# Products of zeros behind the first projection and the second conditioning are left out

## The reference

```python
# layer 0
h = x * rsqrt(mean(x**2)) * (ln1_w * (1 + cond @ ln1_tw.T))
q, k, v = h @ Wq.T, h @ Wk.T, h @ Wv.T      # 8 query heads, 1 key/value head of 64
q, k = rope(q), rope(k)
x = x + softmax(q @ k.T / 8) @ v @ Wo.T
h = x * rsqrt(mean(x**2)) * (ln2_w * (1 + cond @ ln2_tw.T))
x = x + (silu(h @ Wg.T) * (h @ Wu.T)) @ Wd.T # inner width 2048
# layer 1
scale, shift = split(cond @ W_ada.T + b_ada)
h = layernorm(x) * (1 + scale) + shift
q, c = h @ Wq1.T, h @ Wkd.T                  # 16 query heads of 32, latent 128
k, v = c @ Wku.T, c @ Wvu.T                  # 4 key/value heads
x = x + softmax(mask(rope(q) @ rope(k).T / sqrt(32))) @ v @ Wo1.T
```

## Time and profile before

| | |
|---|---|
| time, median of 3 runs | 905.38 us (902.44 to 907.66) |
| the profiled execution's own time | 901.88 us |
| its span, first to last instruction | 900.1 us |
| TensorE busy | 878.1 us (98%) |
| VectorE, ScalarE, GpSimd busy | 63%, 52%, 46% |
| mean granted TensorE clock | 0.998 of 2.4 GHz |
| HBM read, written | 67.96 MB, 4.19 MB |

### The profile page before, as it was taken

How to read it: one execution, slowest core, us unless ns; L and a number is a source line. 1 busy time by engine, 2 the same in 40 slices (tenths; PEclk the granted TensorE clock), 3 DMA queues, 4 the chain that set the end, 5 groups by cost and what they waited for, 6 DMA issues and landing times.

```text
span 900.1 us, 16086 instructions
## 1 busy us (share of the span) xinstructions
PE 878.1 (98%) x6190; PEld 736.7 (82%) x6190; DVE 569.8 (63%) x943; ACT 470.2 (52%) x862; POOL 414.8 (46%) x315
## 2 busy tenths in 40 slices
PE   8898999999999999999999999999999999998997
PEld 5787888888888888887887888888888888888885
DVE  5775556556556556567456676585774765757886
ACT  5666446455445445445537556455464464444662
POOL 3566545445435445446447545453444344431331
PEclk9999999999999999999999999999999999999999
DMA  9901222122222221122132222221222222100001
GB/s 343 333 24 40 103 81 82 71 82 83 71 83 83 71 82 72 71 71 88 71 117 71 71 71 83 71 83 52 68 83 71 83 83 71 69 3 13 25 25 36
DMA packets 31003, 73.19 MB, mean 81 GB/s; under 512 B 4304, under 2 KB 4816, under 8 KB 30928
## 3 DMA queue, kind: packets, MB, share of 16 engines
q1 hardware_dynamic: 30208, 72.07, 23.0%
q10 hardware_dynamic: 720, 0.09, 0.1%
HBM read 67.96 MB, written 4.19 MB: 80 GB/s over the span
## 4 chain that ended last, share of the span: by engine, by line
PE 83%; issue 6%; DVE 5%; POOL 4%; ACT 2%; DMA 0%; POOLq 0%; ACTq 0%; DVEq 0%
PE ps L484 25%; PE ps L486 24%; PE ps L485 24%; PE ps L763 2%; PE ps L590 1%; PE ps L572 1%; PE ps L741 1%; PE ps L751 1%; PE ps L557 1%; POOL qr L343 1%; PE ps L717 1%; POOL qr L395 1%; PE ps L690 1%; POOL stat L317 1%; POOL kr L394 1%
## 5 line engine op out<-in xcount | busy, mean ns | idle before, releaser
L360 POOL TENSOR_TENSOR gul<-rgu,guh 128x1024 fp32r<-128x1024 f32 x64 | 156.4, 2444 | 187.8 <-ACT guh L1453 187.8
L1067 DVE TENSOR_TENSOR xres<-ps,xres 128x512 f32<-128x512 f32 x256 | 174.6, 687 | 88.2 <-PE ps L486 88.2
L484 PE MATMUL ps<-h2h,guh 128*128 128x512 f32 x512 | 205.8, 402 | 0.7 <-issue 0.7
L486 PE MATMUL ps<-h2l,guh 128*128 128x512 f32 x512 | 199.7, 390 | 0.0
L485 PE MATMUL ps<-h2h,gul 128*128 128x512 f32 x512 | 199.5, 390 | 0.0
L486 PEld LDWEIGHTS ps<-h2l,guh 128*128 128x128 f32 x512 | 96.1, 188 | 20.8
L484 PEld LDWEIGHTS ps<-h2h,guh 128*128 128x128 f32 x512 | 96.2, 188 | 20.3 <-issue 1.1
L485 PEld LDWEIGHTS ps<-h2h,gul 128*128 128x128 f32 x512 | 96.3, 188 | 18.7
L484 PE MATMUL ps<-wdh,ah 128*128 128x512 f32 x256 | 101.0, 394 | 1.2 <-DVE al L1062 1.2
L1475 ACT CAST ah<-af 128x512 fp32r<-128x512 f32 x64 | 39.7, 621 | 119.2 <-DVE af L1080 119.2
L486 PE MATMUL ps<-wdl,ah 128*128 128x512 f32 x256 | 99.8, 390 | 0.0
(11 more groups left out here) (172 smaller groups left out, 1688.7 us busy)
## 6 DMA issues: line engine op xcount, KB each, us to landing
rgu<-gu SPq DMA_DIRECT2D x64, 512.0 KB, 3.6
rwd<-WdT SPq DMA_DIRECT2D x64, 256.0 KB, 2.7
xt<-xT SPq DMA_DIRECT2D x16, 256.0 KB, 3.1
out<-xres SPq DMA_DIRECT2D x15, 256.0 KB, 2.3
xres<-x SPq DMA_DIRECT2D x1, 2560.0 KB, 16.2
adaw<-adaT SPq DMA_DIRECT2D x1, 2048.0 KB, 10.3
wst<-WqkvT SPq DMA_DIRECT2D x4, 320.0 KB, 6.0
adaw<-ln_twT SPq DMA_DIRECT2D x4, 256.0 KB, 4.2
```

Of the source, the lines that this page charges most:

```text
L360: pool.tensor_tensor(gul[i][:, :], rgu[i][:, :], guh[i][:, :], ALU.subtract).then_inc(m_gul, 1)
L484: pe.matmul(dst, lh, rh, start=start, stop=False)
L486: return pe.matmul(dst, lh, rl, start=False, stop=stop)
L1067: dve.tensor_tensor(at, bank(BD[i % 2]), at, ALU.add).then_inc(m_x, 1)
```

## The change

Five products of zeros of the beginning are left out: the three behind the first projection and the two behind the second conditioning. Those in front of these places (the four at the start, one between the parts of the first conditioning, three behind its transpose) stay.

```diff
@@ -841,7 +841,6 @@
                     scores(s)
                 if s == -1:
                     first_qkv()
-                    keep_warm(3)
                 elif in_layer(s + 1):
                     qkv(s + 1)
                 if s <= HEAD and in_layer(s - 1):
@@ -853,8 +852,6 @@
                 if s == HEAD + 1:
                     project(s - 1)
                 condition_later(s)
-                if s == -1:
-                    keep_warm(2)
                 fill(pieces, f1)
                 if in_layer(s):
                     p_T(s)
```

## The result

| | before | after |
|---|---|---|
| median | 904.54 us (20 runs, 902.32 to 907.66) | 906.42 us (20 runs, 905.43 to 909.10) |
| ratio | | 1.0025 (95% interval 1.0017 to 1.0033) |
| profiled execution, own time | 901.88 us | 905.94 us |
| its span | 900.1 us | 904.1 us |
| its mean granted TensorE clock | 0.998 | 0.992 |

The change costs 0.25%: about 2.3 us by the ratio, 1.9 us by the medians.

What follows compares the result with a forecast made beforehand. TensorE, busy 98% of the span, was taken as the bound, though off the path where the products stood. Direct effect 0 plus 1.0 us of low clock on the 905.4 us median gave 906.4 us; range 902.5 to 910.

Steps and rivals of the forecast that it cites:

- No direct effect: Program start: the conditioning comes forward 0.0 to 0.5 us, the transposes still wait for GpSimd; gain on the chain 0.
- The clock falls after the longer idle piece: After 2.5 to 2.9 us idle before the first transposes, TensorE drops to 1.2 GHz, beginning between 18.5 and 22.3.
- The price of the low stretch, +1.0 us: First tile's chain: one 3.42 us low-clock stretch costs 0 to +1.3 us, taken as +1.0; two in a row +2.5.
- The first 0.2 us are free.: Second tile's projection: a delay of it alone hides 0.2 us behind VectorE's softmax product, which ends at 26.20.
- The transposes' share, between x1 and x1.8: First tile's transposes, 0.76 us at full clock, slow by x1 to x1.8 at low clock: 0 to +0.6 us.
- The delay passes on: Beyond 25.93 the second tile's rotation, GpSimd's sums and transposes at 30.56 inherit the delay; TensorE then ends late.
- Rival A: Program start: the clock never falls, so cost 0 and time 905.4 us; chance 0.20.
- The forecast: Whole kernel: one or two low-clock stretches, 0 to +2.5 us, expected +1.0, median 906.4 us; chance 0.65.
- Rival B: First tiles: low clock lasts from 20.24 beyond 27 without a break, +5 us, time 910.4; chance 0.10.
- my sign for B: Profile after: the low clock level being there beyond 27 us would show it staying low for several tiles.
- Rival C: First tile: GpSimd's sum L343 speeds up without the products beside it, 0.56 us back, time 904.8; chance 0.05.

Runs made afterwards that it cites:

- the second layer's place out of play: Seven identity products fill TensorE's 2.03 us idle piece at 822 us: kernel before with it 0.9984, changed kernel with it 1.0013, both against the kernel before.
- without the last two: Kernel before with only the two products of zeros behind the second conditioning left out: 1.0021, median 905.85 us.
- more products: Kernel before with five instead of two products of zeros behind the second conditioning: 0.9999, median 904.27 us.
- the changed kernel with the second place filled: Changed kernel with six identity products behind the third conditioning, ahead of the second tile's transposes, against the kernel before: 1.0009, median 906.13 us.

## Why the prediction was right, and where it was off

By the steps of the prediction:

- **No direct effect.** Right. The transposes started at 20.22 for 20.24, ScalarE's copy at 19.17 for 19.19, and the conditioning came forward to 16.22 and was released by its load, at the early one of the two ends that I gave.
- **The clock falls after the longer idle piece.** Right, and the experiments bear it out. In the five profiles with 2.7 us or more of idling ahead of the first transposes (2.71, 2.92, 2.95, 3.09, 4.01) the clock falls there; in the seven with 1.7 us or less it doesn't. Longer pieces mostly go with fewer products; what tells the two apart is that two products or none, with the same 2.9 us of idling, lose the same.
- **The price of the low stretch, +1.0 us.** Right in kind, too small in size. I took one stretch; the profile has two in a row, which I had priced at 2.5 us and which cost 2.69: transposes +0.43 (the copy of the queries starts at 21.47 for 21.04), scores +0.44 (22.11 to 23.17, for 21.68 to 22.30), projection +1.82 (23.17 to 28.62, for 22.30 to 25.93). In it the products stand 0.27 us apart (24.40 to 24.67, for 0.15).
- **"The first 0.2 us are free."** Wrong. Before, the rotation began 0.20 us after the projection's end, and after the change it began 0.20 us after its end too (28.82 - 28.62). What I read as the softmax's cover is the time from TensorE's last product to VectorE's start; both ends fell together by chance. In the sum this is 0.2 us at most.
- **The transposes' share, between x1 and x1.8.** L558 took 0.42 us for 0.27. The Trainium skill's rule ("TensorE: Matmul & The Clock Gate", Part 4), by which they would not change with the clock, does not hold here; by it 0.43 us of the 2.69 would be missing.
- **The delay passes on.** Right, and it grew, which I had not foreseen: 2.69 to 3.68 us at the third tile, by the low stretch at 33.9. Rival A's argument, that 1.78 us of idling behind dense work keep the clock, held for the kernel before and for the four others with that length; the four profiles with 2.05 us or more there all lose it. In the changed kernel that idle piece is 2.06 us, because the work in front of it is done sooner after the projection (the third conditioning starts 0.64 us behind the start of L503, for 0.91 before, when the transposes between them still had to wait for the softmax), while the chain through VectorE and GpSimd is as long as ever (28.82 to 33.25, for 26.13 to 30.56: 4.43 us in both).
- **The forecast.** 906.4 us against a measured 906.42. This agreement owes something to luck: I put +1.0 us on the median of three runs, 905.38, and the median of 20 is 904.54. Measured against that, the price was 1.9 us, 2.3 by the ratio, 2.6 with the second layer's place out of play. The step that failed is the number of low stretches: the term was one. The two profiles differ by three. Over all executions the mean clock is 0.9952 before and 0.9913 after, a difference of two stretches, and with the second layer's place filled it is 0.9970 and 0.9925, a difference of 2.4.
- **Rival B** (several tiles at the low level) did not happen, though not by much: the first low piece ended at 27.05, just where I had put the point from which it would decide, and read to the letter my sign for B, a low level beyond 27, was met by 0.05 us and by the stretch at 33.9. The clock did come back between the two. Only with the later stretch did the profile's loss come near the 4.5 us.
- **Rival C** (GpSimd's sum gets faster) did not happen: L343 takes 1.97 us with the products beside it and without them.

The Trainium skill ("TensorE: Matmul & The Clock Gate", "Terms") prices a low clock roughly as its time by the missing share. By that, as an estimate, the two stretches would cost 6.83 x 0.5 = 3.4 us. The trace shows 2.69: 0.68 us of the time is a wait, and the products slow down by less than a factor of two (the scores from 0.62 to 1.06 us, the projection's products from 0.15 to 0.27 us apart). What is not settled: how often the second tile's idle piece loses the clock in the mean of executions, why the same 2.03 us of idling in the second layer lose it in five profiles and keep it in four, and what decides over the low stretch at the program's end.

## What to carry to other kernels

That TensorE idles behind a product of zeros does not make the product free to take away: look at the granted clock behind the nearest idle piece of that length in the same trace, and price what hangs on the chain in the first microseconds after it. When such products stand behind one another with a load's wait between them, those in front keep those behind in place; what matters is how long TensorE idles just ahead of the next link of the chain. One profile is one execution, and the same idle piece can lose the clock in one and keep it in the next. Look at the mean granted clock of every run before comparing two profiles: an execution with one low stretch fewer can look like a gain of a microsecond, and one without the long stretch at the end like a gain of 2.7.

## What the runs showed of the hardware

- The low stretches of these profiles last 3.4 or 6.8 us. After 2.92 us of idling it was 6.8 us, although TensorE was busy for 6.15 of them; after 2.03, 2.06 and (without the last two) 2.71 us it was 3.4.
- Idling of one length does not always end alike. Ahead of the second tile's transposes 1.78 us kept the clock in five profiles and 2.05 us lost it in four; but the 2.03 us of the second layer lost it in five (of before, after, without the last two, more products, and the changed kernel with the second place filled) and kept it in four. At the program's end the clock fell in seven of twelve profiles with no idle piece over 1.1 us.
- From one profile to the next (each is one execution, of another kernel) the same load took 8.0 to 8.9 us from issue to landing, and landed at 15.2 to 16.2 us. With the five products left out the conditioning started at 16.22 in one profile and at 15.51 in another, where the transposes were 0.4 us later too; the idle piece between them was 2.9 us in the one and 4.0 us in the other:

```profile
15.51 1.08 PE L493 MATMUL ps<-adaw,condt 128*32 128x128 f32 x32
20.61 1.11 PE L557 MATMUL ps<-idn,qr 128*128 128x128 f32 x4 [4.01 <-POOL qr L344]
```

- Products of zeros and products of weights both held the clock at 1.00 in their profiles (ratio 0.9997, 0.9981 to 1.0013).
